# Small VectorE operands held in PSUM, picks behind the search, memory weights behind the second threshold

## The chip, the cores and the metric

The kernel runs on 1 core of one Trainium2 chip. The metric is the device time in microseconds of one execution; lower is better.

## What is computed

Four layers on x of shape (4, 512, 128), each added to x after a layer norm: a diagonal state-space layer, a feed-forward block with FP4-rounded inputs and weights, an attention with 16 heads, and a mixture of 8 experts with a shared block. The change lies in the attention:

```python
dots = einsum('bhij,hk->bkij', q @ k^T * scale, pre_proj)
dots = where(causal, -big, dots)
vk = lax.top_k(dots, 64)[0][..., -1:]
dots = where(dots < vk, -big, dots)
attn = softmax(dots)
attn = einsum('bhij,hk->bkij', attn, post_proj)
out = einsum('bhij,bhjd->bhid', attn, v)
```

Every row of scores (up to 512 keys and 16 memory keys) keeps its 64 largest and is normalised over these.

## The kernel before

`B * H` = 64 passes of attention run in a software pipeline, a pass being one head of one sequence ("head" below). The four tiles `t` of a head are blocks of 128 queries; for the causal mask tile `t` has 144, 272, 400 or 528 columns. All queues are written out by hand in program order; engines meet by semaphores. While VectorE finishes head `g`, it fetches the scores of head `g + 2`.

What happens to a head, with names and lines:

- TensorE makes the scores in PSUM (`scores`, banks `bA` and `bBC`). VectorE fetches them into `Sx`, adds the mask and takes row maxima (`fetch`, L1025), and samples their size (L1031, L1036).
- GpSimd makes a first threshold `cf` (L1304). VectorE counts two tiles against it (`tally`, L1043), ScalarE the other two (`first_tally`, L728). GpSimd corrects the threshold: `moved`, `nthr`, `cf` in `second_threshold` (L1313, L1315, L1317). ScalarE counts again (L736, "second tally"). GpSimd corrects once more (L1323, L1325) and subtracts: `shift`, L1334, four operations, gives `y`, whose sign tells what lies above. ScalarE counts those (`count`, L744) into `over`, and forms the exponentials (`weigh`, L755).
- The count is off 64 by a little. VectorE in `flip` adds a constant of each row, `away = over + steer_s[:, 5]` (L1050), derives sign masks `flips` (L1052) and flips four tiles with them (L1056), so that the sought value is among the 8 largest (L1062, `top`). GpSimd turns `away` into a one-hot `pick` (`pick_last`, L1339 to L1344). TensorE counts the hits of `pick` (`found`, into row 0 of `bA`), VectorE reads them (L1069, L1070).
- VectorE takes the picked value: `picked_top` (L1124), its sum `vk` (L1129), the XOR `yk` (L1134). If hits are missing, `redo_missed` searches a second time (L1078 to L1091). `keep` (L1111) zeroes the exponentials below `yk` and sums; L1114 is the reciprocal `rinv`.
- GpSimd spreads `rinv` on diagonals (`spread`, L1353) and scales the memory columns (`mem_w`, L1357). TensorE turns and scales the weights by matmul with `spread` (L450), ScalarE copies them (L763), TensorE multiplies by the values (L464).

The order on GpSimd for one turn of its loop: `second_threshold(g+1)`, `pick_last(g)`, `stage_memory_keys(g+3)`, `third_threshold(g+1)`, `shift(g+1)`, `first_threshold(g+2)`, `spread_scale(g)`.

## Time and profile before

| | |
|---|---|
| median of 3 runs | 1032.03 us (1031.37 to 1032.18) |
| profiled execution | 1033.08 us, span 1031.4 us |
| busy share: TensorE, VectorE, ScalarE, GpSimd | 88%, 82%, 72%, 46% |
| DMA queues, share of 16 engines | 7.7% (most before the head pipeline) |
| granted TensorE clock, mean of the span | 0.95 |

The profile is of one execution. The span is the time from the first to the last instruction; the small rest of 1.7 us lies around it. Shares are of the whole span, over stages with different limits: the head pipeline runs from about 170 to 855 us, the rest is the layers before and after it. In the timeline a row gives its start, how long it took, the engine, the source line, the operation, the tile written and those read.

### The profile page before, as it was taken

How to read it: one execution, taken by the hardware profiler on the slowest of the kernel's cores; microseconds unless marked ns; L12 is line 12 of the kernel's file. 1: busy time of each engine (PE TensorE's matmuls, PEld its weight loads, DVE VectorE, ACT ScalarE, POOL GpSimd, SP SyncE). 2: the span in 40 equal slices, each digit the busy share in tenths (PEclk: the TensorE clock that was granted, in tenths of full speed). 3: DMA queues.
4: the chain of work that ended last, by engine and by line, in shares of the span. 5: the costliest groups of instructions: out<-in, count | busy, mean ns of one | idle time of the engine just before them, and what ended most of it. 6: DMA issues, size and time to landing. Idle time of an engine off the chain costs nothing.

```text
span 1031.4 us, 16155 instructions
## 1 busy us (share of the span) xinstructions
PE 909.6 (88%) x4151; PEld 581.7 (56%) x4151; DVE 848.0 (82%) x2863; ACT 746.8 (72%) x1932; POOL 471.8 (46%) x1113
## 2 busy tenths in 40 slices
PE   7856777998999998989999999789998789899998
PEld 4523444666666666666666666567666566433432
DVE  4687994999999999999999999989999983446344
ACT  6423236899999999999999999779998883211211
POOL 2000013677676676676766776556765652000000
PEclk9867988899999999999999999989999989899999
DMA  4855310000000000000000000000000000000000
GB/s 155 157 119 92 77 16 1 1 2 2 2 2 2 2 1 2 2 1 2 2 2 2 2 2 2 1 2 2 2 2 1 1 1 1 0 1 10 11 1 21
DMA packets 15006, 18.13 MB, mean 18 GB/s; under 512 B 2657, under 2 KB 12193, under 8 KB 14241
## 3 DMA queue, kind: packets, MB, share of 16 engines
q1 hardware_dynamic: 14880, 16.84, 7.7%
q14 instruction: 93, 0.75, 0.3%
q8 instruction: 33, 0.54, 0.2%
HBM read 11.07 MB, written 5.77 MB: 16 GB/s over the span
## 4 chain that ended last, share of the span: by engine, by line
DVE 48%; PE 28%; issue 11%; ACT 7%; POOL 2%; DVEq 1%; POOLq 1%; DMA 0%; ACTq 0%
DVE Ex L1111 11%; DVE top L1062 7%; DVE mixed L1056 6%; DVE Sx L1025 4%; DVE unread L1043 3%; PE bH L464 3%; DVE yk L1134 2%; PE bFGI L450 2%; PE bBC L559 2%; PE bA L559 2%; DVE away L1050 2%; PE bFGI L568 2%; PE bFGI L560 2%; PE bBC L560 2%; PE bH L568 2%
## 5 line engine op out<-in xcount | busy, mean ns | idle before, releaser
L1334 POOL TENSOR_TENSOR mixed<-Sx,nthr 128x528 f32<-128x528 f32 (+3 forms) x256 | 185.8, 757 | 11.5 <-issue 11.5
L450 PEld LDWEIGHTS bFGI<-spread,Ex 128*128 128x128 f32 x1280 | 157.4, 202 | 58.9 <-POOL spread L1353 57.5
L464 PE MATMUL bH<-turned 128*128 128x512 f32 (+3 forms) x512 | 152.9, 442 | 36.9 <-ACT turned L763 36.6
L450 PE MATMUL bFGI<-spread,Ex 128*128 128x128 f32 x1280 | 166.8, 289 | 17.4 <-POOL spread L1353 17.4
L736 ACT ACTIVATE unread<-Sx,nthr 128x144 bf16<-128x144 f32 (+3 forms) x256 | 143.9, 563 | 20.2 <-POOL nthr L1315 16.6
L464 PEld LDWEIGHTS bH<-turned 128*128 128x128 f32 x512 | 92.1, 189 | 97.9 <-issue 77.6
L744 ACT ACTIVATE unread<-mixed,least 128x528 bf16<-128x528 f32 (+3 forms) x256 | 143.4, 566 | 0.0
L1111 DVE SCALAR_TENSOR_TENSOR Ex<-mixed,yk,Ex 128x144 f32<-128x144 f32 (+3 forms) x256 | 139.5, 598 | 1.7 <-ACT Ex L755 1.0
L755 ACT ACTIVATE Ex<-Sx,nmax 128x144 f32<-128x144 f32 (+3 forms) x256 | 125.5, 563 | 0.0
L1062 DVE MAX8 top<-mixed 128x8 f32<-128x528 f32 (+3 forms) x256 | 110.8, 493 | 0.0
L1353 POOL TENSOR_TENSOR spread<-ident,rinv 128x512 f32<-128x512 f32 x64 | 66.5, 1039 | 84.1 <-DVE rinv L1114 84.1
L728 ACT ACTIVATE unread<-Sx,cf 128x400 bf16<-128x400 f32 (+1 forms) x128 | 85.7, 673 | 9.1 <-POOL cf L1304 9.1
L1056 DVE TENSOR_SCALAR mixed<-mixed,flips 128x528 int32<-128x528 int32 (+3 forms) x256 | 84.0, 390 | 2.3
L763 ACT ACTIVATE turned<-bFGI 128x1280 f32<-128x1280 f32 x64 | 77.8, 1216 | 11.0 <-PE bFGI L450 11.0
L1025 DVE CUSTOM_DVE_ANT_0 Sx<-bBC,causal 128x400 f32<-128x400 f32 (+1 forms) x128 | 79.7, 623 | 0.6 <-PE bBC L441 0.5
L422 PE MATMUL bE<-per_head,xn 128*128 128x128 f32 x512 | 76.9, 295 | 0.0
L441 PE MATMUL bBC<-Y,xn 128*128 128x512 f32 x128 | 71.7, 642 | 0.0
L422 PEld LDWEIGHTS bE<-per_head,xn 128*128 128x128 f32 x512 | 64.6, 198 | 7.9 <-issue 0.9
L415 PE MATMUL bE<-xn,per_head 128*128 128x512 f32 x128 | 65.5, 593 | 1.6 <-DVE xr L986 1.6
L438 PE MATMUL bA<-Y,xn 128*128 128x144 f32 (+1 forms) x256 | 57.4, 348 | 1.4 <-ACT Y L721 0.8
L1290 POOL COPY um_turned<-per_head 128x256 f32<-128x256 f32 x1 | 0.7, 736 | 126.4 <-DMA per_head<-mixed_store 126.4
L839 ACT ACTIVATE Ex<-bBC 128x512 f32<-128x512 f32 x24 | 14.3, 597 | 57.0 <-PE bFGI L560 57.0
(346 smaller groups left out, 1797.7 us busy)
## 6 DMA issues: line engine op xcount, KB each, us to landing
heads_store<-per_head SPq DMA_DIRECT2D x2, 1152.0 KB, 5.0
mixed<-heads_store SPq DMA_DIRECT2D x16, 144.0 KB, 10.8
mixed_store<-mixed SPq DMA_DIRECT2D x2, 1152.0 KB, 4.2
per_head<-mixed_store SPq DMA_DIRECT2D x16, 144.0 KB, 6.0
xr<-in_xT SPq DMA_DIRECT2D x4, 256.0 KB, 3.5
w_s<-in_w12T SPq DMA_DIRECT2D x1, 1024.0 KB, 13.9
outT<-xc SPq DMA_DIRECT2D x4, 256.0 KB, 2.0
wq_s<-in_WqT SPq DMA_DIRECT2D x1, 512.0 KB, 4.2
```

The lines of the kernel that those rows point to most:

```text
L422: done = mm(bE[:, jt * P:jt * P + P], xn[:, b, jt * P:jt * P + P], Bw[:, h, :], start=True, stop=True)
L450: last = mm(bFGI[:, k * P:k * P + P], Ex[g % 2][:, t, a:a + P], spread[:, t, :], start=True, stop=True)
L464: last = mm(bH[:, jt * P:T], u[:, jt, :], PT[:, at:at + n], start=h + jt == 0, stop=False)
L728: last = nc.scalar.activation(unread[1][:, OFF[t]:OFF[t] + NT[t]], Sx[g % 2][:, t, 0:NT[t]], ACT.Sign, bias=cf[g % 2][:, 0, t:t + 1], accu ...
L736: last = nc.scalar.activation(unread[0][:, OFF[t]:OFF[t] + NT[t]], Sx[g % 2][:, t, 0:NT[t]], ACT.Sign, bias=nthr[g % 2][0][:, t:t + 1], ac ...
L744: last = nc.scalar.activation(unread[2][:, OFF[t]:OFF[t] + NT[t]], y[g % 2][t], ACT.Sign, bias=least[:, :], accum_out=over[g % 2][:, t:t + 1])
L755: nc.scalar.activation(Ex[g % 2][:, t, 0:NT[t]], Sx[g % 2][:, t, 0:NT[t]], ACT.Exp, bias=nmax[g % 2][:, t:t + 1], scale=1 / DOWN).then_inc ...
L1025: V.tensor_tensor_reduce(out=Sx[g % 2][:, t, 0:NT[t]], in0=scores_in[t], in1=causal[:, W - NT[t]:W], scale=DOWN, scalar=LOW, op0=ALU.add, ...
L1056: V.tensor_scalar(near[t].bitcast(I32), y[g % 2][t].bitcast(I32), flips[:, t:t + 1], None, ALU.bitwise_xor).then_inc(sem("flipped"), 1)
L1062: last = V.max(top[:, t, :], near[t])
L1111: V.scalar_tensor_tensor(Ex[g % 2][:, t, 0:NT[t]], y[g % 2][t], yk[:, t:t + 1], Ex[g % 2][:, t, 0:NT[t]], ALU.is_ge, ALU.mult, accum_out=r ...
L1334: Gp.tensor_tensor(y[ph][t], Sx[ph][:, t, 0:NT[t]], nthr[ph][1][:, t:t + 1].broadcast_to((P, NT[t])), ALU.add).then_inc(sem("y_ready"), 1)
```

## The change

A region of 4 columns of PSUM bank `bA` beside the scores of tiles 0 and 1 holds the constants of `away` (`steer_p`, copied once at the start), and another 4 columns the picked sum (`vk_p`). `flip` waits for the scores of head `g + 2` in `bA` first. The picked product and its sum come directly behind the hits; `yk` stands behind the first fetch, the other fetches behind `yk`. On GpSimd `mem_w` becomes a step of its own, `weigh_memory(g - 1)`, behind `second_threshold(g + 1)`. The second search forms `vk` again from `yk` by one more XOR and drain.

```diff
--- before.py
+++ after.py
@@ -203,6 +203,8 @@
         quad = [bA[:, :], bBC[:, 0:512], bBC[:, 512:1024], bI]
         scores_in = [bA[:, 0:NT[0]], bA[:, OFF[1]:OFF[1] + NT[1]], bBC[:, 0:NT[2]], bBC[:, 512 - MEM:1024]]
         hits_in = bA[0:1, 512 - 2 * TT * WIN:512].rearrange("p (t k) -> p t k", t=TT)
+        steer_p = bA[:, OFF[2]:OFF[2] + TT]
+        vk_p = bA[:, OFF[2] + TT:OFF[2] + 2 * TT]
         ln4_bank = [bBC[:, 0:512], bBC[:, 512:1024], bA[:, :], bF]
         half_bank = [(bBC[:, 0:512], bI), (bA[:, :], bBC[:, 512:1024])]
         ln3_bank = [bH[:, :], bF, bG, bI]
@@ -576,7 +578,7 @@
                 if g == HEADS:
                     wide4(0)
                     wide4(1)
-                    pe.wait_ge(sem("hits_read"), HEADS)
+                    pe.wait_ge(sem("yk_ready"), HEADS)
                     mean4(2)
                 if 0 <= g < HEADS:
                     found(g)
@@ -1046,8 +1048,10 @@
 
             def flip(g):
 
+                if g + 2 < HEADS:
+                    dve.wait_ge(sem("s_done"), 3 * (g + 2) + 1)
                 dve.wait_ge(sem("counted"), g + 1)
-                V.tensor_tensor(away[:, :], over[g % 2][:, :], steer_s[:, 5, :], ALU.add).then_inc(sem("away_ready"), 1)
+                V.tensor_tensor(away[:, :], over[g % 2][:, :], steer_p, ALU.add).then_inc(sem("away_ready"), 1)
                 dve.wait_ge(sem("away_ready"), g + 1)
                 V.tensor_scalar(flips[:, :], away[:, :].bitcast(I32), REST, TWO, ALU.bitwise_or, ALU.bitwise_xor).then_inc(sem("flips_ready"), 1)
                 dve.wait_ge(sem("flips_ready"), g + 1)
@@ -1085,6 +1089,8 @@
                     V.tensor_tensor(further[:, :, :], pick[:, :, WIN:2 * WIN], further[:, :, :], ALU.mult)
                     dve.drain()
                     V.tensor_reduce(vk_far[:, :], further[:, :, :], AX.X, ALU.add)
+                    dve.drain()
+                    V.tensor_tensor(vk[:, :].bitcast(I32), yk[:, :].bitcast(I32), flips[:, :], ALU.bitwise_xor)
                     dve.drain()
                     V.tensor_tensor(vk[:, :], vk[:, :], vk_far[:, :], ALU.add)
                     dve.drain()
@@ -1120,21 +1126,25 @@
 
             def pick_tops(g):
 
+                dve.wait_ge(sem("pick_ready"), g + 1)
                 dve.wait_ge(sem("topped"), 2 * g + 2)
                 V.tensor_tensor(picked_top[:, :, :], pick[:, :, 0:WIN], top[:, :, :], ALU.mult).then_inc(sem("top_picked"), 1)
 
             def add_tops(g):
 
                 dve.wait_ge(sem("top_picked"), g + 1)
-                V.tensor_reduce(vk[:, :], picked_top[:, :, :], AX.X, ALU.add).then_inc(sem("vk_ready"), 1)
+                V.tensor_reduce(vk_p, picked_top[:, :, :], AX.X, ALU.add).then_inc(sem("vk_ready"), 1)
 
             def last_kept(g):
 
                 dve.wait_ge(sem("vk_ready"), g + 1)
-                V.tensor_tensor(yk[:, :].bitcast(I32), vk[:, :].bitcast(I32), flips[:, :], ALU.bitwise_xor).then_inc(sem("yk_ready"), 1)
+                V.tensor_tensor(yk[:, :].bitcast(I32), vk_p.bitcast(I32), flips[:, :], ALU.bitwise_xor).then_inc(sem("yk_ready"), 1)
 
             for g in range(-2, HEADS):
                 there, coming = 0 <= g, g + 2 < HEADS
+                if g == 0:
+                    V.tensor_copy(steer_p, steer_s[:, 5, :]).then_inc(sem("steer_moved"), 1)
+                    dve.wait_ge(sem("steer_moved"), 1)
                 if there:
                     flip(g)
                     nearest(g, (3, 2))
@@ -1145,20 +1155,15 @@
                     if g > H and g % H == 1:
                         take_sum(g // H - 1)
                     read_hits(g)
+                    pick_tops(g)
+                    add_tops(g)
                 if coming:
                     free_for_fetch(g + 2)
                     fetch(g + 2, (0,))
                 if there:
-                    pick_tops(g)
-                if coming:
-                    fetch(g + 2, (1,))
-                if there:
-                    add_tops(g)
-                if coming:
-                    fetch(g + 2, (2,))
-                if there:
                     last_kept(g)
                 if coming:
+                    fetch(g + 2, (1, 2))
                     measure_first(g + 2)
                     fetch(g + 2, (3,))
                 if there:
@@ -1352,6 +1357,11 @@
                     pool.wait_ge(sem("turned_all"), g)
                 Gp.tensor_tensor(spread[:, :, :], ident[:, :].unsqueeze(1).broadcast_to((P, TT, P)),
                                  r[:, :].unsqueeze(2).broadcast_to((P, TT, P)), ALU.mult).then_inc(sem("spread_ready"), 1)
+
+            def weigh_memory(g):
+
+                b, h = divmod(g, H)
+                r = rinv[g % 2]
                 if h == 0 and b:
                     pool.wait_ge(sem("memT_done"), b)
                 Gp.tensor_tensor(mem_w[:, :, h, :], Ex[g % 2][:, :, 0:MEM], r[:, :].unsqueeze(2).broadcast_to((P, TT, MEM)), ALU.mult).then_inc(sem("mem_ready"), 1)
@@ -1359,6 +1369,8 @@
             for g in range(-3, HEADS):
                 if 0 <= g + 1 < HEADS:
                     second_threshold(g + 1)
+                if g >= 1:
+                    weigh_memory(g - 1)
                 if g >= 0:
                     pick_last(g)
                 if g + 3 < HEADS:
@@ -1375,6 +1387,7 @@
                                          rstd[:, TT * b:TT * b + TT].unsqueeze(2).broadcast_to((P, TT, P)), ALU.mult).then_inc(sem("ln_diag"), 1)
                 if g >= 0:
                     spread_scale(g)
+            weigh_memory(HEADS - 1)
             for b in range(B):
                 pool.wait_ge(sem("ln_root"), max(b, 1) + 1)
                 Gp.tensor_tensor(diag4[b].rearrange("p (t n) -> p t n", t=TT), ident[:, :].unsqueeze(1).broadcast_to((P, TT, P)),
```

GpSimd, the steady loop, from `spread` to the pick, before:

```order
L1353 TENSOR_TENSOR spread<-ident,rinv 128x512
L1357 TENSOR_TENSOR mem_w<-Ex,rinv 128x4x16
L1313 TENSOR_TENSOR moved<-above,cf 128x4
L1315 TENSOR_TENSOR nthr_0<-moved,cf 128x4
L1317 TENSOR_TENSOR cf<-nthr_0,cf 128x4
L1339 TENSOR_TENSOR away<-away 128x4
L1341 TENSOR_TENSOR pick<-odd,away 128x64
L1344 TENSOR_SCALAR pick<-pick 128x64
```

and now:

```order
L1358 TENSOR_TENSOR spread<-ident,rinv 128x512
L1318 TENSOR_TENSOR moved<-above,cf 128x4
L1320 TENSOR_TENSOR nthr_0<-moved,cf 128x4
L1322 TENSOR_TENSOR cf<-nthr_0,cf 128x4
L1367 TENSOR_TENSOR mem_w<-Ex,rinv 128x4x16
L1344 TENSOR_TENSOR away<-away 128x4
L1346 TENSOR_TENSOR pick<-odd,away 128x64
L1349 TENSOR_SCALAR pick<-pick 128x64
```

`mem_w` has gone from between `spread` and `moved` to between `cf` and `away` (the square of VectorE's `away`).

VectorE, from the search for the 8 largest to the third fetch (`ISA` with a tile is a fetch, `ISA rmax` reads its maximum), before:

```order
L1062 MAX top<-mixed 128x8 x4
L1069 TENSOR_REDUCE hits<-bA 1x1
L1070 TENSOR_REDUCE hits<-bA 1x4
L1025 ISA Sx,rmax<-bA,causal 128x144
L1025 ISA rmax 128x1
L1124 TENSOR_TENSOR picked_top<-pick,top 128x32
L1025 ISA Sx,rmax<-bA,causal 128x272
L1025 ISA rmax 128x1
L1129 TENSOR_REDUCE vk<-picked_top 128x4
L1025 ISA Sx,rmax<-bBC,causal 128x400
L1025 ISA rmax 128x1
L1134 TENSOR_TENSOR yk<-vk,flips 128x4
```

and now:

```order
L1066 MAX top<-mixed 128x8 x4
L1073 TENSOR_REDUCE hits<-bA 1x1
L1074 TENSOR_REDUCE hits<-bA 1x4
L1131 TENSOR_TENSOR picked_top<-pick,top 128x32
L1136 TENSOR_REDUCE bA<-picked_top 128x4
L1027 ISA Sx,rmax<-bA,causal 128x144
L1027 ISA rmax 128x1
L1141 TENSOR_TENSOR yk<-bA,flips 128x4
L1027 ISA Sx,rmax<-bA,causal 128x272
L1027 ISA rmax 128x1
L1027 ISA Sx,rmax<-bBC,causal 128x400
L1027 ISA rmax 128x1
```

The product L1124 and the sum L1129 have come in front of the first fetch (now L1131, L1136), and the sum goes to `bA`; the XOR `yk` reads `bA` and stands in front of the second fetch.

## Rows read from the trace of the kernel before

**Rows 1.** Timeline, VectorE L1114: first and last of 62 reciprocals (start us, us, engine line op out<-in xcount).
```profile
198.27 0.18 DVE L1114 RECIPROCAL rinv<-rsum 128x4 f32<-128x4 f32 x1
...
844.26 0.18 DVE L1114 RECIPROCAL rinv<-rsum 128x4 f32<-128x4 f32 x1
```

**Rows 2.** Timeline, ScalarE, one head of the longer kind, 569.5 to 579.8.
```profile
569.52 0.62 ACT L728 ACTIVATE unread<-Sx,cf 128x400 bf16<-128x400 f32 x1
...
571.83 0.41 ACT L736 ACTIVATE unread<-Sx,nthr 128x144 bf16<-128x144 f32 x1 [0.29 <-POOL nthr L1315]
...
579.76 0.62 ACT L728 ACTIVATE unread<-Sx,cf 128x400 bf16<-128x400 f32 x1
```

**Rows 3.** Timeline, GpSimd, the same head (last bracket: idle before, releaser).
```profile
569.54 1.04 POOL L1353 TENSOR_TENSOR spread<-ident,rinv 128x512 f32<-128x512 f32 x1 [0.91 <-DVE rinv L1114]
570.54 0.29 POOL L1357 TENSOR_TENSOR mem_w<-Ex,rinv 128x64 f32<-128x64 f32 x1
571.09 0.36 POOL L1313 TENSOR_TENSOR moved<-above,cf 128x4 f32<-128x4 f32 x1 [0.25 <-ACT unread L728]
...
571.95 0.31 POOL L1317 TENSOR_TENSOR cf<-nthr,cf 128x4 f32<-128x4 f32 x1 [0.16 <-issue]
...
573.01 0.38 POOL L1344 TENSOR_SCALAR pick<-pick 128x64 f32<-128x64 f32 x1 [0.16 <-issue]
...
574.98 2.97 POOL L1334 TENSOR_TENSOR mixed<-Sx,nthr 128x528 f32<-128x528 f32 x4 [0.18 <-issue]
```

**Rows 4.** Timeline, VectorE, the same head.
```profile
569.28 0.18 DVE L1114 RECIPROCAL rinv<-rsum 128x4 f32<-128x4 f32 x1
...
570.05 0.55 DVE L1050 TENSOR_TENSOR away<-over,steer_s 128x4 f32<-128x4 f32 x1
570.64 0.22 DVE L1052 TENSOR_SCALAR flips<-away 128x4 int32<-128x4 int32 x1
570.90 1.31 DVE L1056 TENSOR_SCALAR mixed<-mixed,flips 128x528 int32<-128x528 int32 x4
...
573.77 0.16 DVE L1069 TENSOR_REDUCE hits<-bA 1x1 int32<-1x32 f32 x1
...
575.26 0.80 DVE L1134 TENSOR_TENSOR yk<-vk,flips 128x4 int32<-128x4 int32 x1
...
579.53 0.18 DVE L1114 RECIPROCAL rinv<-rsum 128x4 f32<-128x4 f32 x1
```

**Rows 5.** Timeline, VectorE L1056: the second and the fourth flip of Rows 4 by themselves.
```profile
571.31 0.42 DVE L1056 TENSOR_SCALAR mixed<-mixed,flips 128x400 int32<-128x400 int32 x1
...
571.91 0.29 DVE L1056 TENSOR_SCALAR mixed<-mixed,flips 128x144 int32<-128x144 int32 x1
```

**Rows 6.** Timeline, GpSimd and ScalarE, one head of the shorter kind.
```profile
550.91 0.20 POOL L1313 TENSOR_TENSOR moved<-above,cf 128x4 f32<-128x4 f32 x1
551.25 0.20 POOL L1315 TENSOR_TENSOR nthr<-moved,cf 128x4 f32<-128x4 f32 x1
...
551.49 0.41 ACT L736 ACTIVATE unread<-Sx,nthr 128x144 bf16<-128x144 f32 x1
```

**Rows 7.** Timeline, the head of 383.76: VectorE, GpSimd, ScalarE.
```profile
385.38 1.31 DVE L1056 TENSOR_SCALAR mixed<-mixed,flips 128x528 int32<-128x528 int32 x4
...
385.88 0.39 POOL L1313 TENSOR_TENSOR moved<-above,cf 128x4 f32<-128x4 f32 x1 [0.57 <-ACT unread L728]
386.42 0.33 POOL L1315 TENSOR_TENSOR nthr<-moved,cf 128x4 f32<-128x4 f32 x1
...
386.78 0.42 ACT L736 ACTIVATE unread<-Sx,nthr 128x144 bf16<-128x144 f32 x1 [0.76 <-POOL nthr L1315]
```

**Rows 8.** Timeline, VectorE, a head in which GpSimd is idle there.
```profile
353.38 0.17 DVE L1050 TENSOR_TENSOR away<-over,steer_s 128x4 f32<-128x4 f32 x1 [1.46 <-ACT unread L744]
353.58 0.17 DVE L1052 TENSOR_SCALAR flips<-away 128x4 int32<-128x4 int32 x1
```

**Rows 9.** Groups by line and form, 200 to 800: line engine op, count | busy us, mean ns.
```profile
L1025 DVE CUSTOM_DVE_ANT_0 Sx<-bBC,causal 128x528 f32<-128x528 f32 x57 | 39.4, 692 | 0.0
```

## The prediction

> **What bounds the kernel now.** I read the table of engine shares first, then the timeline of one head after another in the stretch where 64 heads run in a pipeline. A head is counted from one reciprocal (L1114) to the next. From the reciprocal at 198.27 to the one at 844.26 there are 61 intervals [rows 1]; ten are longer than 10.5 us (two sequence changes, three heads that search a second time with the heads behind them, and a few more) and take 127.7 us together. The other 51 take 645.99 - 127.7 = 518.3 us, 10.16 us each. They come in two kinds, and one place tells them apart: the start of ScalarE's second tally (L736).
>
> In the longer kind the tally waits 0.29 us for GpSimd's `nthr` [rows 2]. ScalarE starts its first tally at 569.52 and the next head's at 579.76, 10.24 us later; of that it works all but this wait, so in these heads ScalarE, held by GpSimd, sets the pace. GpSimd's `moved` starts 571.09 - 569.52 = 1.57 after the first tally began, takes 0.36 and not 0.20 [rows 3]. In the shorter kind `moved` and `nthr` both take 0.20, the chain from `moved` to L736 is 0.58 and not 0.74 [rows 6], and a head takes 0.16 less, some 10.09.
>
> Why 0.36? While `moved` runs, VectorE is in its four flips (L1056) [rows 4]. The operation began 0.19 after the first flip and ended 0.55 after it, just after the flip did; one that begins together with the first flip (at +0.01 in the shorter kind) or between two flips passes freely. The same is seen at the fourth flip: `cf` begins 0.04 after it and takes 0.31, not 0.20 [rows 3, 5]. In the other direction `away` (0.17 alone) takes 0.55 and ends at 570.60, 0.02 after `spread` on GpSimd; `flips` takes 0.22 where it takes 0.17 alone, and ends 0.03 after `mem_w`; the last XOR `yk`, on four columns like `away`, takes 0.80 under the first piece of GpSimd's shift, begun 0.28 before it [rows 3, 4, 8]. So each engine holds the other off until its instruction ends.
>
> **The change part by part, times from a head's reciprocal R.**
>
> *`away` with its constants in PSUM.* It has one SBUF input left. I take it at its free 0.17: from R+0.77 to 0.94, against 1.32 before. Next is `flips`, at R+0.98. The price naively is -0.40. But `spread` holds GpSimd from R+0.26 to R+1.30, and `flips` is an operation that `mem_w` held up. So I take `flips` to end 0.03 after `spread`, at R+1.33, and the flips to start at R+1.36, where they now start at R+1.62: a gain of 0.26. The bounds are 0 (PSUM frees nothing) and 0.44 (`flips` escapes, start R+1.18).
> The Trainium skill, SBUF — State Buffer, section Who interferes with whom, says that the shared port pair is exclusive, that a tensor_tensor with both inputs in SBUF contends with GpSimd's reads, and that tensor_scalar from SBUF to SBUF in its 2-port form takes the pair too. By that rule the freed `away` hands its wait to `flips`, as I took it; without it the sum would have R+1.18. The 0.22 against 0.17 agrees.
>
> *`mem_w` behind the second threshold.* One 0.29 us operation leaves the place after `spread` and adds about 0.25 between `cf` and the pick. It did not delay `moved`: its end, 570.83, lies before ScalarE's release at 571.09 [rows 3]. So no gain there; its removal is what lets `flips` go right after `spread`. Behind the pick wait TensorE's count and VectorE's hits, now 573.77, 0.38 after the pick's end [rows 3, 4]. With the pick later and VectorE 0.26 earlier, VectorE waits there, about 0.5 us of idle time. It is not on the path: the keep behind it cannot finish before GpSimd's shift, which ends at 577.95; the next reciprocal is 1.58 later [rows 3, 4]. From L736 to the next reciprocal is 7.70 [rows 2, 4], and I keep that.
>
> *Picks directly behind the hits, `vk` in PSUM.* Same instructions, in another order. `picked_top` and its sum now depend on each other with nothing between them: +0.1. `yk` no longer waits for the shift: -0.6 (0.80 to about 0.17). The keep then arrives some 0.2 earlier than now, at the same shift: nothing. The new semaphore wait at the head of `flip` is for scores that TensorE finished well before, zero; cover: were TensorE late, `flip` and everything behind it would wait. The one copy of the constants falls where VectorE first waits for ScalarE, zero. The extra XOR and drain in the second search cost 0.2 in three heads.
>
> *What earlier flips meet.* This is the term that decides. Longer heads follow one another with the first tally at R+0.24, so `moved` asks at R+1.81. The flips start at R+1.36; the second, 0.41 later [rows 4, 5], at R+1.77. So `moved` asks 0.45 after the first flip and 0.04 after the second: the phase in which `cf` is held at the fourth flip. The head of 383.76 shows nearly this case. There the flips start at 385.38, `moved` asks 0.50 later and takes 0.39, `nthr` starts at 386.42, 1.04 after the flips began, meets the fourth flip and takes 0.33, and L736 starts at 386.78: 1.40 after the flips began [rows 7]. With that, L736 starts at R + 1.36 + 1.40 = R+2.76, against 2.55 (571.83 - 569.28) in the longer kind now and 2.21 in the shorter.
>
> A head then takes 2.76 + 7.70 = 10.46 us, and the phase repeats itself: ScalarE's work from L736 to the next first tally is 579.76 - 571.83 = 7.93 [rows 2], so the next first tally comes again 0.23 after the next reciprocal, whatever the wait was. The sum: 51 x (10.46 - 10.16) = +15.3 us, and -1 for the ten other intervals, where VectorE is the late one and loses its waits. Net +14.3 us. The profiled execution took 1033.08 with a span of 1031.4; the median of the runs is 1032.03. The difference put on the median gives 1046.
>
> **The rivals.**
> *The gaps are met.* `moved` slips in between first and second flip, and `nthr` between two later ones. Then `moved` runs from R+1.81 to 2.01, `nthr` from 2.15 to 2.35, L736 starts at R+2.39, and every head takes 2.39 + 7.70 = 10.09 us: 51 x (10.09 - 10.16) - 1 = -4.6, 1027.5. It decides at about 0.04 us: `moved` has to ask before the second flip begins. For it: `nthr` passes freely at 551.25, 0.35 after that head's flips began. Against it: `cf` at the fourth flip, held at the same 0.04.
> *`flips` escapes `spread`.* The flips start at R+1.18. `moved` at +0.63 ends with the second flip, near +0.89, `nthr` asks at +1.03 and meets the fourth, L736 at R+1.18+1.40 = 2.58. A head takes 10.28: 51 x 0.12 - 1 = +5, 1037. Against it stands the 0.22 of `flips` beside `mem_w`.
> *PSUM frees nothing.* `away` still ends with `spread`, at R+1.32, and `flips` follows in 0.17: the flips start at R+1.56, `moved` (at +0.25) is held until +0.55, which is R+2.11, `nthr` runs from 2.25 to 2.45, L736 is at R+2.50. A head takes 10.20: +2, and `yk` keeps its wait, so 1034. Against it: the last fetch (L1025), which reads scores in PSUM and the mask in SBUF, runs under the shift in nearly every head and takes 0.69 on the mean of 57, so such a pair does not wait [rows 9].
>
> **How the numbers follow.** Forecast 0.60; gaps 0.19; escape 0.12; nothing freed 0.09. A measurement of this kernel tells 0.2%, 2 us, from no change. Faster is the gaps, 0.19. Same, 0.13, is most of the case in which nothing is freed and the part of the escape in which `nthr` also gets through. Slower is the rest, 0.68. For the forecast alone the range is 1040 to 1049: the lower end if `moved` is held and `nthr` is not (L736 at R+1.36+0.89+0.14+0.20+0.04 = R+2.63, 10.33 a head, 51 x 0.17 - 1 = +7.7), the upper with 0.06 more in each head. The whole range takes in the rest of the chance, to the gaps: 1028 to 1049.
>
> **What would show it.** In the profile after: `away` near 0.17; `flips` some 0.35 long, ending just after `spread`; `moved` and `nthr` longer than 0.20, both; ScalarE idle before L736 of about 0.5 per head; `yk` near 0.17; VectorE idle before the hits of 0.3 to 0.6; reciprocals 10.4 to 10.5 apart. I am wrong if reciprocals are 10.1 apart and `moved` takes 0.20, or if `flips` takes 0.17 under `spread`.

## The result and the profile after

The changed kernel takes 1042.4 us (median of 5 runs, 1038.23 to 1043.94), the kernel before, five runs beside them, 1032.03 (1031.37 to 1033.22): a ratio of 1.0095, 95% interval 1.0082 to 1.0107. It is slower by 10.4 us; 14 were forecast.

The profiled execution is the shortest of the five, 1038.23 us with a span of 1036.5. The profile pages, sections 4 (the chain that ended last) and 5 (groups of instructions: busy us, mean ns, idle us before them and its main cause). The kernel before:

```profile
DVE 48%; PE 28%; issue 11%; ACT 7%; POOL 2%; DVEq 1%; POOLq 1%; DMA 0%; ACTq 0%
...
L736 ACT ACTIVATE unread<-Sx,nthr 128x144 bf16<-128x144 f32 (+3 forms) x256 | 143.9, 563 | 20.2 <-POOL nthr L1315 16.6
```

The changed kernel:

```profile
ACT 45%; PE 25%; issue 11%; DVE 10%; POOLq 5%; POOL 2%; DVEq 1%; DMA 0%; ACTq 0%
...
L738 ACT ACTIVATE unread<-Sx,nthr 128x144 bf16<-128x144 f32 (+3 forms) x256 | 143.9, 563 | 31.6 <-POOL nthr L1320 31.3
L1117 DVE SCALAR_TENSOR_TENSOR Ex<-mixed,yk,Ex 128x144 f32<-128x144 f32 (+3 forms) x256 | 153.9, 653 | 1.7 <-ACT Ex L757 1.0
```

ScalarE now leads the chain that ended last. Its second tally (L738; L736 before) is as long as before, 143.9 us in all, but ScalarE idles 31.6 us ahead of it and not 20.2, nearly all of it for `nthr`. These 11.4 us more are about what the regular heads lose.

The first and the last reciprocal of the pipeline that [rows 1] are compared with, and the very last one (timeline of VectorE, changed kernel):

```profile
198.62 0.18 DVE L1120 RECIPROCAL rinv<-rsum 128x4 f32<-128x4 f32 x1
...
853.99 0.18 DVE L1120 RECIPROCAL rinv<-rsum 128x4 f32<-128x4 f32 x1
...
862.21 0.18 DVE L1120 RECIPROCAL rinv<-rsum 128x4 f32<-128x4 f32 x1
```

The 61 intervals took 645.99 us and now take 655.37, 9.4 more. The two kinds of head are gone: of the 51 intervals that were regular before, 48 are now 10.41 or 10.42 us. The span grew by only 5.1, since this execution's part after the last reciprocal was 4.3 shorter (174.3 us; 178.6 before, from a last reciprocal at 852.76). In the profiled executions of all the kernels below that part came out anywhere between 174 and 179 us, and the part ahead of the pipeline, up to the reciprocal that [rows 1] start with, between 196.4 and 203.2. The edits all stand in the pipeline, but for one wait of TensorE at its end. So I judge each kernel by its pipeline too, from that reciprocal to the last (654.5 us before, 663.6 after); there is one profile of each kernel.

One head of the changed kernel, R = 398.33, on GpSimd, ScalarE and VectorE (timeline; start, duration, then what ended idle time). It answers to [rows 2 to 4]:

```profile
398.59 1.04 POOL L1358 TENSOR_TENSOR spread<-ident,rinv 128x512 f32<-128x512 f32 x1 [0.90 <-DVE rinv L1120]
400.19 0.39 POOL L1318 TENSOR_TENSOR moved<-above,cf 128x4 f32<-128x4 f32 x1 [0.56 <-ACT unread L730]
400.72 0.33 POOL L1320 TENSOR_TENSOR nthr<-moved,cf 128x4 f32<-128x4 f32 x1
401.21 0.20 POOL L1322 TENSOR_TENSOR cf<-nthr,cf 128x4 f32<-128x4 f32 x1 [0.16 <-issue]
401.37 0.29 POOL L1367 TENSOR_TENSOR mem_w<-Ex,rinv 128x64 f32<-128x64 f32 x1
...
402.41 0.38 POOL L1349 TENSOR_SCALAR pick<-pick 128x64 f32<-128x64 f32 x1 [0.16 <-issue]
```

```profile
398.61 0.62 ACT L730 ACTIVATE unread<-Sx,cf 128x400 bf16<-128x400 f32 x1
...
401.09 0.41 ACT L738 ACTIVATE unread<-Sx,nthr 128x144 bf16<-128x144 f32 x1 [0.46 <-POOL nthr L1320]
```

```profile
398.33 0.18 DVE L1120 RECIPROCAL rinv<-rsum 128x4 f32<-128x4 f32 x1
...
399.10 0.15 DVE L1054 TENSOR_TENSOR away<-over,bA 128x4 f32<-128x4 f32 x1
399.29 0.37 DVE L1056 TENSOR_SCALAR flips<-away 128x4 int32<-128x4 int32 x1
399.69 0.49 DVE L1060 TENSOR_SCALAR mixed<-mixed,flips 128x528 int32<-128x528 int32 x1
...
403.15 0.18 DVE L1073 TENSOR_REDUCE hits<-bA 1x1 int32<-1x32 f32 x1 [0.51 <-PE bA L473]
...
403.98 0.16 DVE L1141 TENSOR_TENSOR yk<-bA,flips 128x4 int32<-128x4 int32 x1
...
406.23 0.65 DVE L1117 SCALAR_TENSOR_TENSOR Ex<-mixed,yk,Ex 128x144 f32<-128x144 f32 x1
```

What to see: `away` is free (0.15, 0.55 before), `flips` behind it takes its wait (0.37) and ends at 399.66, 0.03 after `spread`. The four flips start at R+1.36. `moved` asks at R+1.86, under the second flip, and takes 0.39; `nthr` meets the fourth and takes 0.33; the second tally starts at R+2.76. The next reciprocal is at 408.74, R+10.41. `yk` is free at 0.16, the first keep is not: 0.65 where it takes 0.36 in the head of [rows 4].

### The profile page after: what moved, and what is told of

Same layout as the page of the kernel before. It is cut to its first block, busy times and chain, and to the rows that moved or that the text cites. A ratio compares the mean times of both kernels' runs of the same rounds, so it can differ in the third digit from the quotient of the medians.

```text
span 1036.5 us, 16288 instructions
## 1 busy us (share of the span) xinstructions
PE 900.2 (87%) x4151; PEld 579.6 (56%) x4151; DVE 833.0 (80%) x2867; ACT 746.7 (72%) x1932; POOL 487.2 (47%) x1113
## 4 chain that ended last, share of the span: by engine, by line
ACT 45%; PE 25%; issue 11%; DVE 10%; POOLq 5%; POOL 2%; DVEq 1%; DMA 0%; ACTq 0%
ACT Ex L757 10%; ACT unread L746 10%; ACT unread L738 9%; ACT unread L730 7%; ACT turned L765 6%; ACT turned L772 2%; PE bBC L561 2%; POOLq L1319 2%; PE bA L561 2%; PE bFGI L570 2%; POOLq L1321 2%; PE bFGI L562 2%; PE bFGI L452 2%; PE bBC L562 2%; PE bH L570 2%
## 5 line engine op out<-in xcount | busy, mean ns | idle before, releaser
L452 PE MATMUL bFGI<-spread,Ex 128*128 128x128 f32 x1280 | 160.8, 283 | 17.1 <-POOL spread L1358 16.9
L738 ACT ACTIVATE unread<-Sx,nthr 128x144 bf16<-128x144 f32 (+3 forms) x256 | 143.9, 563 | 31.6 <-POOL nthr L1320 31.3
L1117 DVE SCALAR_TENSOR_TENSOR Ex<-mixed,yk,Ex 128x144 f32<-128x144 f32 (+3 forms) x256 | 153.9, 653 | 1.7 <-ACT Ex L757 1.0
L757 ACT ACTIVATE Ex<-Sx,nmax 128x144 f32<-128x144 f32 (+3 forms) x256 | 125.6, 564 | 0.0
L440 PE MATMUL bBC<-Y,xn 128*128 128x400 f32 x128 | 54.8, 511 | 0.0
```

The lines of the kernel that those rows point to most:

```text
L440: last = mm(scores_in[t], x_t, k[:, 0:NT[t]], start=True, stop=True)
L452: last = mm(bFGI[:, k * P:k * P + P], Ex[g % 2][:, t, a:a + P], spread[:, t, :], start=True, stop=True)
L738: last = nc.scalar.activation(unread[0][:, OFF[t]:OFF[t] + NT[t]], Sx[g % 2][:, t, 0:NT[t]], ACT.Sign, bias=nthr[g % 2][0][:, t:t + 1], ac ...
L757: nc.scalar.activation(Ex[g % 2][:, t, 0:NT[t]], Sx[g % 2][:, t, 0:NT[t]], ACT.Exp, bias=nmax[g % 2][:, t:t + 1], scale=1 / DOWN).then_inc ...
L1117: V.scalar_tensor_tensor(Ex[g % 2][:, t, 0:NT[t]], y[g % 2][t], yk[:, t:t + 1], Ex[g % 2][:, t, 0:NT[t]], ALU.is_ge, ALU.mult, accum_out=r ...
```

## The experiments

**H** is the theory of the forecast: what counts is where `moved` and `nthr` fall among the four flips. **L**: the pick, moved behind the memory weights and waited for by the hits, delays the rest of the head. **S**: the operations that now read and write PSUM are themselves slow, or (where an expectation says so) some path is only shifted in length. Every kernel was measured with runs of the kernel before beside it, whose median came out between 1029.57 and 1032.14 us, so medians of different rows compare only roughly and the ratio is the fair number. Even the executions of one kernel lie in groups: those with two memsets at 1023.3 to 1024.8 and 1029.1 to 1030.2 us, the median between them. "Head" is the mean, in the profile, of the 51 intervals that are regular in the kernel before, "pipeline" the time from the reciprocal of [rows 1] to the very last one.

| kernel | us, median | ratio to before, interval | head | pipeline |
|---|---|---|---|---|
| before | 1032.03 | | 10.16 | 654.5 |
| changed | 1042.4 | 1.0095, 1.0082 to 1.0107 | 10.39 | 663.6 |
| constants alone | 1036.03 | 1.0039, 1.0022 to 1.0056 | 10.31 | 659.4 |
| memory weights alone | 1033.89 | 1.0026, 1.0012 to 1.0041 | 10.30 | 659.5 |
| picks alone | 1029.67 | 0.9993, 0.9976 to 1.001 | 10.19 | 654.3 |
| changed, constants back | 1027.95 | 0.998, 0.9957 to 1.0003 | 10.16 | 652.3 |
| changed, memory weights back | 1030.88 | 1.0025, 0.9997 to 1.0054 | 10.26 | 656.6 |
| changed, 1 memset | 1045.08 | 1.0113, 1.0067 to 1.0159 | 10.41 | 665.6 |
| changed, 2 memsets | 1026.95 | 0.9942, 0.9924 to 0.996 | 10.09 | 648.7 |
| changed, 3 memsets | 1029.6 | 0.9985, 0.9959 to 1.0011 | 10.12 | 651.0 |
| changed, 4 memsets | 1031.63 | 1.0005, 0.9988 to 1.0021 | 10.19 | 655.2 |
| changed, 2 memsets, memory weights back | 1025.52 | 0.996, 0.9933 to 0.9987 | 10.14 | 650.8 |
| changed, flips and MAX8 in turn | 1029.55 | 0.9982, 0.9967 to 0.9998 | 10.12 | 651.7 |
| before, flips and MAX8 in turn | 1078.77 | 1.0459, 1.0438 to 1.0479 | 11.14 | 704.2 |

**One part at a time.** The constants alone, on the kernel before (the one copy of the constants, not shown, is in it too):

```diff
+                if g + 2 < HEADS:
+                    dve.wait_ge(sem("s_done"), 3 * (g + 2) + 1)
...
-                V.tensor_tensor(away[:, :], over[g % 2][:, :], steer_s[:, 5, :], ALU.add)...
+                V.tensor_tensor(away[:, :], over[g % 2][:, :], steer_p, ALU.add)...
```

> The kernel before with the constants of away in PSUM and nothing else. Theory H (held operations: GpSimd's moved and nthr meet VectorE's flips in a worse phase): away takes 0.16, flips ends just after spread, the flips start near R+1.36 to 1.45; mem_w, right behind spread, may stretch the first flip by 0.1. moved asks near R+1.81 to 1.86, at the start of the second flip, and is held in most heads: heads of 10.3 to 10.45 us, total 1038 to 1046. If the stretched first flip puts the gap just there, heads of 10.1 and 1029. Theory L (the later pick makes VectorE wait for its hits, and that is the loss): the pick is not later here, so no loss, 1028 to 1032. Theory S (small operands in PSUM are slow to use): a loss of a few us at away itself, which would then take more than 0.2.

A longer head of it, R = 452.09 (timelines of VectorE and GpSimd):

```profile
452.86 0.15 DVE L1053 TENSOR_TENSOR away<-over,bA 128x4 f32<-128x4 f32 x1
453.05 0.37 DVE L1055 TENSOR_SCALAR flips<-away 128x4 int32<-128x4 int32 x1
453.45 0.50 DVE L1059 TENSOR_SCALAR mixed<-mixed,flips 128x528 int32<-128x528 int32 x1
```

```profile
453.93 0.42 POOL L1319 TENSOR_TENSOR moved<-above,cf 128x4 f32<-128x4 f32 x1 [0.28 <-ACT unread L729]
454.49 0.34 POOL L1321 TENSOR_TENSOR nthr<-moved,cf 128x4 f32<-128x4 f32 x1
```

Part of the loss is there with this part alone, with the mechanism of the forecast: flips at R+1.36, `moved` and `nthr` held. The pipeline is 4.9 us longer, of the 9.1 of the whole change, and 1036.03 lies below the 1038 to 1046 that I expected. The heads of the shorter kind are still there, about half of all: their first tally starts at R+0.06, `moved` asks 0.28 after the flips began, takes 0.27 or 0.28 and leaves with the first flip, `nthr` is free, and the second tally starts at R+2.30. `mem_w` still stands behind `spread` here, and `flips` slips in ahead of it all the same. So the memory weights had not to move for the flips to start at R+1.36; that sentence of the forecast is wrong.

The memory weights alone: the lines of `weigh_memory` as in the change, `away` with its constants in SBUF.

```diff
+                if g >= 1:
+                    weigh_memory(g - 1)
                 if g >= 0:
                     pick_last(g)
```

> The kernel before with the memory weights behind the second threshold and nothing else. Theory H: away still ends with spread, flips then takes 0.17 and the flips start at R+1.56; moved is held to R+2.11, L736 at R+2.50: heads of 10.1 to 10.2, total 1028 to 1034. Theory L: the pick is 0.25 later, VectorE waits for its hits and the kernel loses 5 to 15 us: 1037 to 1047.

`away` takes 0.55, `flips` 0.17, the flips start at R+1.56, and the second tally at R+2.50, as expected. The heads are not the 10.1 to 10.2 us that I expected: about half take 10.20, the others 10.39. One of the latter, R = 400.69, on VectorE and GpSimd:

```profile
402.25 1.31 DVE L1056 TENSOR_SCALAR mixed<-mixed,flips 128x528 int32<-128x528 int32 x4
```

```profile
402.34 0.47 POOL L1313 TENSOR_TENSOR moved<-above,cf 128x4 f32<-128x4 f32 x1 [0.34 <-ACT unread L728]
```

In the kernel before, `moved` of a shorter head asks at R+1.63, 0.01 or 0.02 after the flips began, and passes [rows 6]. Here the flips begin 0.06 earlier, it asks 0.09 after them and is held until 0.56, with the first flip. So the pass that made the shorter kind short is gone, and this too is H. In this head the first keep is held too (0.54 and not 0.36), so that from L736 to the next reciprocal it is 7.89 us and not 7.70. But that is so in many heads of the kernel before as well (keep 0.55, 7.88 us), and is nothing new. The whole takes 2.0 us more than the kernel before beside it (1031.86), the pipeline 5.0.

The picks alone: `pick_tops` and `add_tops` behind `read_hits`, the sum in PSUM, the rest as before.

> The kernel before with the picks directly behind the hits and the picked sum in PSUM, constants and memory weights as before. Theory H: the flips start at R+1.62 as before, yk takes 0.16, every head becomes one of the longer kind (moved held by the first flip, L736 at R+2.55) and 10.20 us: 1032 to 1035. Theory L: no later pick, no loss. Theory S: the sum into PSUM and the XOR out of it cost 0.1 or more each and show in every head, 1036 or more.

Heads of 10.19 or 10.20 as expected, with `moved` at 0.31 in most of them; no measurable change (1029.67, 2 below the range that I expected). `yk` takes 0.16: reading and writing the sum in PSUM costs nothing that shows, against S.

**The change with one part undone.** First the constants, `steer_s[:, 5, :]` in the place of `steer_p`, without the copy and the wait for `s_done`; memory weights and picks stay changed:

```diff
-                V.tensor_tensor(away[:, :], over[g % 2][:, :], steer_p, ALU.add)...
+                V.tensor_tensor(away[:, :], over[g % 2][:, :], steer_s[:, 5, :], ALU.add)...
```

> The changed kernel with the constants of away back in SBUF, all else as changed (later pick, picks behind the hits, picked sum in PSUM). Theory H: away takes 0.55 again and pushes the flips back to R+1.56; moved is held to R+2.11 and nthr passes, L736 at R+2.50, heads of 2.50 + 7.65 = 10.15 us: the loss is gone, 1029 to 1033. Theory L: the pick is as late as in the change, the loss stays, 1040 to 1044. Theory S: part of the loss stays, since the picked sum is still in PSUM.

```profile
448.91 0.49 DVE L1057 TENSOR_SCALAR mixed<-mixed,flips 128x528 int32<-128x528 int32 x1
...
449.18 0.29 POOL L1312 TENSOR_TENSOR moved<-above,cf 128x4 f32<-128x4 f32 x1 [0.52 <-ACT unread L729]
449.61 0.20 POOL L1314 TENSOR_TENSOR nthr<-moved,cf 128x4 f32<-128x4 f32 x1
```

These are rows of its head R = 447.35 (VectorE, GpSimd). `moved` asks 0.27 after the flips began, not 0.50, and leaves with the first of them; `nthr` is free. With the later pick and the sum in PSUM both still there, the loss is gone (1027.95, 1 below the expected range; heads mostly of 10.17). L falls as the main cause. The wait for `s_done`, which went away together with the constants, isn't the cause either: `away` starts at R+0.77 with it and without it.

Then the memory weights, back directly behind `spread`:

```diff
-                if g >= 1:
-                    weigh_memory(g - 1)
...
+                Gp.tensor_tensor(mem_w[:, :, h, :], Ex[g % 2][:, :, 0:MEM], ...).then_inc(sem("mem_ready"), 1)
```

> The changed kernel with the memory weights back in their old place, directly behind spread: the constants and the picks are left of the change. H: flips start at R+1.36 as in the run of the constants alone, so moved and nthr are held in the heads where ScalarE's first tally starts at R+0.24 to 0.28 (L738 at R+2.76), and partly free where it starts at R+0.06 (L738 at R+2.30). With the picks ahead of the shift, yk no longer waits, the keep comes early and is held by the third piece of the shift: R+2.76 + 7.65 = 10.41, and the next head's first tally at R+0.28: the longer kind follows itself, all heads at 10.41, 1040 to 1043 us. If the picks come so early that the shorter kind can hold itself as with the constants alone (10.0 and 10.2), the mean is 10.2 to 10.3, 1031 to 1037. Additive rival (each part has its own price, constants +4, memory weights +2.7, picks -0.7): 1032.1 + 3.3 = 1035.

Head R = 457.19, GpSimd and ScalarE, and its first keep on VectorE:

```profile
459.21 0.24 POOL L1318 TENSOR_TENSOR moved<-above,cf 128x4 f32<-128x4 f32 x1 [0.47 <-ACT unread L730]
459.59 0.34 POOL L1320 TENSOR_TENSOR nthr<-moved,cf 128x4 f32<-128x4 f32 x1
```

```profile
459.96 0.41 ACT L738 ACTIVATE unread<-Sx,nthr 128x144 bf16<-128x144 f32 x1 [0.31 <-POOL nthr L1320]
```

```profile
464.86 0.36 DVE L1117 SCALAR_TENSOR_TENSOR Ex<-mixed,yk,Ex 128x144 f32<-128x144 f32 x1
```

The second tally is still at R+2.77, but a head takes 10.26 and not 10.41. The pick comes 0.25 earlier, the first keep starts at R+7.67 and not R+7.90, ahead of the shift's third piece, and takes 0.36 and not 0.65. From the second tally to the next reciprocal it is 7.50 us, which I had not expected. The reciprocal, and with it the flips, so come earlier against ScalarE: `moved` asks at R+2.02, later under the second flip, and waits less for the same end. So L holds in part: within the whole change the later pick costs 0.15 per head, 51 x 0.15 = 7.7 us, but through the meeting with the flips. 1030.88 lies near the 1031 to 1037 of my second branch, which got there by another way. Of the pipeline's 9.1 us, the memory weights are worth 663.6 - 656.6 = 7.0 by this run, and the constants 663.6 - 652.3 = 11.3 by the run before it. They are not additive.

**Idle work between `flips` and the four flips.** If the phase decides, time spent doing nothing on VectorE must make the kernel faster at some lengths and not at others:

```diff
                 dve.wait_ge(sem("flips_ready"), g + 1)
+                V.memset(idle[:, 0:64], 0.0)
+                V.memset(idle[:, 64:128], 0.0)
```

Two memsets, then four:

> The changed kernel with two idle operations (VectorE sets 64 unused columns to zero, twice) between flips and the four flips of every head: more work for VectorE, nothing else changed. Theory H: the flips start later by the time of the two, to near R+1.5. moved asks at R+1.86, 0.34 to 0.36 after the first flip, is held for next to nothing, and nthr meets the gap behind the second flip: L736 near R+2.45, heads of 10.1 us instead of 10.42, total 1027 to 1032, faster although VectorE does more. If the delay is only 0.1, nthr is held by the third flip and a head takes 10.3. Theory L and theory S: more work on VectorE in front of the hits leaves the time the same or makes it longer, 1042 to 1048.

> The same with four idle operations. Theory H: the flips start near R+1.65 to 1.75; moved asks 0.1 to 0.2 after the first flip and is held until it ends (0.55 after its start), nthr passes: L736 at R+2.55 to 2.7, heads of 10.2 to 10.35 us, total 1033 to 1040: slower than with two operations, still faster than the change. Theories L and S: 1042 or more.

Then one and three:

> The changed kernel with one memset of 64 idle columns between flips and the four flips. H (the phase of the flips decides): two of them moved the flips from R+1.36 to R+1.51, so one puts them at R+1.43 to R+1.44. moved asks at R+1.85, 0.41 to 0.42 after they start, which is where the second flip begins (0.41 after the first). This is the edge itself. If moved slips in before the second flip it takes 0.20, L738 starts near R+2.43, and a head takes 10.1 us, 1027 us. If the second flip is ahead of it, moved is held to R+2.32, nthr meets the fourth flip, L738 starts at R+2.76 to 2.83, a head takes 10.4 to 10.5 us, 1040 to 1046 us; in that case one memset more than the change is slower or equal and two are 15 us faster, which no theory that counts VectorE's work can give. In the short of it: 10.1 or 10.4 to 10.5, nothing between. S (it is only the length of some path that the memsets shift by chance): half of the way from 1042 to 1027, 1034.

> The same with three. H: the flips start at R+1.58 to R+1.59, moved asks at R+1.82 to 1.85, under the first flip, and is released 0.55 after the start of the flips, at R+2.13 to 2.14; nthr is free, L738 at R+2.51, a head takes 10.16 to 10.18 us (as with constants_back, whose flips start at R+1.56: 10.17), 1028 to 1030 us, between the two (1027) and four (1032) memsets.

The first flip, `moved`, `nthr` and the second tally, with one memset (R = 444.77) and with two (R = 447.35), from the timelines of VectorE, GpSimd and ScalarE. One memset:

```profile
446.21 0.42 DVE L1062 TENSOR_SCALAR mixed<-mixed,flips 128x528 int32<-128x528 int32 x1
...
446.62 0.40 POOL L1320 TENSOR_TENSOR moved<-above,cf 128x4 f32<-128x4 f32 x1 [0.55 <-ACT unread L731]
447.17 0.33 POOL L1322 TENSOR_TENSOR nthr<-moved,cf 128x4 f32<-128x4 f32 x1
...
447.54 0.41 ACT L739 ACTIVATE unread<-Sx,nthr 128x144 bf16<-128x144 f32 x1 [0.47 <-POOL nthr L1322]
```

Two memsets:

```profile
448.75 0.11 DVE L1059 MEMSET idle<- 128x64 f32 x1
448.83 0.11 DVE L1060 MEMSET idle<- 128x64 f32 x1
448.86 0.43 DVE L1063 TENSOR_SCALAR mixed<-mixed,flips 128x528 int32<-128x528 int32 x1
...
449.20 0.20 POOL L1321 TENSOR_TENSOR moved<-above,cf 128x4 f32<-128x4 f32 x1 [0.55 <-ACT unread L731]
449.54 0.20 POOL L1323 TENSOR_TENSOR nthr<-moved,cf 128x4 f32<-128x4 f32 x1
...
449.78 0.41 ACT L739 ACTIVATE unread<-Sx,nthr 128x144 bf16<-128x144 f32 x1
```

In both ScalarE gives its total at R+1.85. With one memset the first flip has run 0.41 by then, the second is about to begin, and `moved` loses 0.20 and `nthr` 0.13. With two the first flip has run 0.34; `moved` goes in front of the second flip and loses nothing, and no idle time is shown before ScalarE's tally. From 0, 1, 2, 3 and 4 memsets a regular head mostly takes 10.42, 10.43, 10.09, 10.14 and 10.21 us. The second memset, 0.08 us of extra work, takes 18 us off the kernel (1045 to 1027; 17 in the pipeline), and the next two, 0.15 us, give 5 back. No theory that counts work does this. Three came out as expected in the time, with the head 0.02 shorter; four at 1031.63, below the 1033 to 1040 that I expected. In both an operation held at the first flip is released 0.48 or 0.49 after the flips began and not 0.55, since that flip behind a memset takes 0.42. Two memsets make a kernel that beats the kernel before, by 0.4 to 0.8%.

**Both savings together.** Memory weights back (10.26 a head) and two memsets (10.09):

> Two edits that each made the changed kernel faster, together: the memory weights back in their old place (alone: a head of 10.26 us, 1031 us) and two memsets of 64 idle columns before the four flips (alone: 10.09, 1027 us). H: the flips start at R+1.51. With the memory weights back the keep comes at L738 + 4.9, ahead of the third piece of the shift, and is free, so L738 to the next reciprocal is 7.50 and the next head's first tally starts at R+0.43, not at R+0.28. moved then asks at R+2.00, 0.49 after the flips began and so under the second flip; it is held to R+2.40, nthr asks at R+2.54, where the fourth flip begins, and takes 0.33, L738 starts at R+2.92 and a head takes 10.42 us: as slow as the changed kernel, 1040 to 1044 us. Additive rival (each saving keeps its size: 0.33 and 0.16 off 10.42): 9.93 us a head, 1018 us. Rival that ScalarE's own loop is the floor (1.57 + 0.58 + 7.93 = 10.08) and nothing more is held: 10.08, 1026 us.

The profile holds both of a pair of regimes. From 384 to 446 us a head takes 10.33: `moved` asks at R+2.02, under the second flip. Rows of R = 415.01, GpSimd and ScalarE:

```profile
417.03 0.31 POOL L1321 TENSOR_TENSOR moved<-above,cf 128x4 f32<-128x4 f32 x1 [0.47 <-ACT unread L731]
417.48 0.34 POOL L1323 TENSOR_TENSOR nthr<-moved,cf 128x4 f32<-128x4 f32 x1
...
417.85 0.41 ACT L739 ACTIVATE unread<-Sx,nthr 128x144 bf16<-128x144 f32 x1 [0.38 <-POOL nthr L1323]
```

Then one keep is 0.06 late (at 446), and from 456 on nearly all regular heads take 10.08 to 10.10: `moved` asks at R+1.86 and is free, and the first keep, at R+7.38, is held and takes 0.83 or 0.84. My expectation of 10.42 was wrong on two counts: the held kind is 10.33, since the first flip behind a memset takes 0.42 and not 0.49 and everything is released 0.07 earlier, and it is not the only one that repeats itself. The additive 9.93 never appears. The rival with a floor at 10.08 gives the time best (1025.52 measured, 1026 by it), though the head of the profile, 10.14 on the mean, isn't all at the floor. The two savings together win nothing over two memsets alone: the ratios are 0.996 and 0.9942, the pipelines 650.8 and 648.7. ScalarE's own loop is 1.57 from its first tally to `moved` [rows 2, 3], 0.58 to the second tally when nothing is held [rows 6] and 7.93 to the next first tally [rows 2], 10.08 in all. In the regular heads the last piece is 7.93 to 7.96 in all fourteen profiles, the first 1.56 to 1.59 in all but the last of the table. So the length of a regular head, from first tally to first tally, is 9.5 us plus what passes from `moved` to the second tally: 0.58 free, 0.90 in the changed kernel, and there 1.57 + 0.90 + 7.94 = 10.41. The kernel before was at 10.16, and so in the 51 regular heads no reordering on VectorE or GpSimd had more than 51 x 0.08 = 4 us to win unless ScalarE's work shrinks too. Two memsets took 3.9 of them; the rest of the 5.8 us that the pipeline got shorter comes from the other intervals.

**Each flip followed by its MAX8**, to open gaps between the flips, in the changed kernel and in the one before:

```diff
-                for t in (3, 2, 1, 0):
-                    dve.wait_ge(sem("y_ready"), TT * g + 4 - t)
-                    V.tensor_scalar(near[t].bitcast(I32), ...)
...
                 for t in tiles:
+                    dve.wait_ge(sem("y_ready"), TT * g + 4 - t)
+                    V.tensor_scalar(near[t].bitcast(I32), ...)
```

> The changed kernel with each flip followed at once by the search for the 8 largest of its tile (which has one input and holds nothing), instead of four flips and then four searches. Theory H: behind the first flip stands 0.7 us of search, so moved (asks at R+1.86, 0.5 after the flip began) and nthr meet no flip and take 0.20 each: L736 near R+2.44, heads of 10.09 us, total 1024 to 1029, faster than both kernels, though VectorE waits for its own results three times more per head (0.2 to 0.4 us, in front of hits for which it waits anyway). Theory L: no gain over the change, the hits come no earlier, 1042. If VectorE's own waits are longer than its cover, heads of 10.2 to 10.3.

> The kernel before with the same interleaving. Theory H: flips start at R+1.62, moved (R+1.63 to 1.86) is held by the first flip at most, nthr never. That is what already holds before, so nothing is won in the kinds of head; VectorE has no cover for its own waits here (its hits are there when it asks), so 0.2 to 0.4 us per head may come onto the path: heads of 10.2 to 10.4, total 1033 to 1045. The comparison with the interleaved changed kernel shows what the change is worth once the flips are out of the way.

In the changed kernel `nthr` is free and `moved` takes 0.20 to 0.30, a head takes 10.05, about every fourth one 10.32; ScalarE's first tallies are mostly 10.09 or 10.10 apart, as expected. The time, 1029.55, is just above the expected 1024 to 1029. The kernel before went the other way, 4.6% slower, which I had not foreseen. Rows of its head R = 453.00, VectorE and then GpSimd:

```profile
457.99 0.16 DVE L1068 TENSOR_REDUCE hits<-bA 1x1 int32<-1x32 f32 x1
...
458.43 1.02 DVE L1123 TENSOR_TENSOR picked_top<-pick,top 128x32 f32<-128x32 f32 x1
...
460.33 0.50 DVE L1133 TENSOR_TENSOR yk<-vk,flips 128x4 int32<-128x4 int32 x1
```

```profile
458.35 2.85 POOL L1333 TENSOR_TENSOR mixed<-Sx,nthr 128x528 f32<-128x528 f32 x4 [0.18 <-issue]
```

`moved` is free there too, and the second tally starts at R+2.20. But the hits come at R+4.99 and not 4.49, and `picked_top`, which takes 0.17 in the changed kernel, starts 0.08 after GpSimd's shift and takes 1.02: the length of the shift's first piece. `yk` is held by the second piece, and the keep begins more than 1 us later: a head takes 11.14 us on the mean and not 10.2 to 10.4. In the changed kernel the same operation stands directly behind the hits, ahead of the shift. So it seems that the picks of this change, worth nothing by themselves, are what made the interleaving safe. That is read from these rows; no run puts the picks alone and the interleaving together.

## Why the prediction was right, and where its sizes were off

- **`away` free, `flips` handed its wait, flips at R+1.36.** Right to 0.02: 0.15, 0.37, R+1.36. It is also what the Trainium skill, SBUF — State Buffer, section Who interferes with whom, leads one to expect: an operand moved to PSUM frees that operation from the shared port pair and not the tensor_scalar behind it. The reason that I gave with it, that `mem_w` had to leave the place behind `spread`, was wrong, as the run of the constants alone shows.
- **`moved` and `nthr` both held, the second tally at R+2.76.** Right, to 0.01, in 48 of the 51 heads, with the first tally at R+0.28 instead of 0.24 and so `moved` asking at R+1.86 instead of 1.81: later under the same flip, with the same end. The runs with one and two memsets show that this is the cause.
- **"From L736 to the next reciprocal is 7.70, and I keep that."** The mis-sized term: 7.65. Counted from the second tally, the keep arrived 0.33 earlier than in the longer kind (5.14 after it, 5.47 before) and was held by the third piece, so that its end moved by 0.04 only. The stretch was no constant of the kernel before either: it is 7.70 where the first keep is free and 7.88 where it is held. So the reciprocals of shorter heads stand 9.92 or 10.09 apart, those of longer ones 10.25 or 10.43. ScalarE's first tallies are 10.09 or 10.25 apart all the same: the keep moves the reciprocal against ScalarE, and so the flips against `moved`. A head takes 10.41 to 10.42, not 10.46: 48 x 0.045 = 2.2 us less. And "nothing" for the later pick was right only in the sum: without it the stretch would have been 7.50.
- **+15.3 for the 51 regular intervals.** They took 529.7 us, 11.5 more than 518.3. 2.2 of the missing 3.8 are the item above. 1.6 are three heads behind second searches, of 9.85, 9.97 and 9.97 where 10.46 was counted.
- **-1 for the ten others.** 125.6 us against 127.7, so -2.1. The sum is 11.5 - 2.1 = 9.4, forecast 14.3.
- **The hits wait for the pick and it costs nothing.** The wait was 0.51 as forecast. That it isn't on the path was wrong: without it a head is 0.15 shorter (10.26, the run with the memory weights back).
- **The rivals.** `flips` did not escape `spread`, and PSUM did free `away`. The gaps were met in the kernel with two memsets: 10.09 a head, as worked out for that rival, at 1026.95 against 1027.5. The agreement is in part luck: the second tally was at R+2.43 or 2.44 and not 2.39, the stretch behind it 7.66 and not 7.70, and no single execution lies between 1024.8 and 1029.1.

One thing stays open. The medians differ by 10.4 us, the pipelines of the two profiled executions by 9.1; the rest lies within what the parts ahead of the pipeline (6.8 us) and behind it (5 us) vary by from profile to profile, and I did not find what makes them vary. That 1046 came within 4 us of the median is therefore worth less than that the head, 10.46, came within 0.05.

## What to carry to other kernels

When two engines hold each other off, a shorter operation moves every later one against the other engine, so work out where each request falls among the other's instructions before counting a saving. Then try a small delay on either side: it costs one run, and here 0.15 us of idle work turned a loss of 1% into a gain of 0.6% over the kernel before. And first add up the loop of the engine that paces the heads: 10.08 of 10.16 us here, which bounds all that such a reordering can win in these heads.

## What was not expected of the hardware

- In every kernel here with four flips in a row, a GpSimd operation held at the flips nearly always ended 0.55, 0.89 or 1.37 us after they began (each to 0.02), and 0.48, 0.82 or 1.30 where memsets stand ahead of them, whenever it asked. These are the ends of the first, the second and the fourth.
- The edge is sharper than 0.08 us: a request 0.34 after the first flip's start passed with 0.20, one 0.41 after it took 0.40. It is the same at the shift: the first keep starting 1.75 us after the shift began took 0.36, one starting 1.80 after it took 0.84.
- An operation of 0.17 us took 1.02 when it started 0.08 behind a GpSimd operation of 528 columns. The price of such a meeting is the rest of the other's instruction, whatever one's own size.
- The first flip behind a memset took 0.42 or 0.43, behind `flips` 0.49 or 0.50.
- The same program can settle in either of two repeating patterns (10.33 and 10.09 us a head) and leave one for the other after a single late operation.
